# Front stage of a two-layer megakernel: ScalarE normalises, the next tile's x is transposed, differenced and mixed earlier, and the masked shifts are written with one tensor each

## The chip, the cores and the metric

The kernel runs on one core of a Trainium2 chip. Its engines are named as in the profile: PE (TensorE matrix multiplies), PEld (its weight loads), DVE (VectorE), ACT (ScalarE), POOL (GpSimd) and SP (SyncE, which here only issues DMAs). The metric is the device time of one execution in microseconds, median over runs.

## The reference

Two layers, each a sequence mixer beside a feed-forward part, on x of 4 x 512 tokens with 512 channels, all in float32. The change is in the front of layer 0, which computes for each batch entry:

```python
xn = (x - mean(x)) / sqrt(var(x) + 1e-5)                 # layer norm over 512 channels
delta = shifted(xn) - xn                                 # previous token minus this one
lr = tanh((xn + delta * mu_x) @ Wx1)                     # 512 -> 5 x 64
mus = einsum('btnr,hnr->btnh', lr, Wx2) + x_bias         # five mixes: r, w, k, v, g
r, k, v = ((xn + delta * m) @ W for m, W in ((mr, Wr), (mk, Wk), (mv, Wv)))
w = tanh((xn + delta * mw) @ Ww_a) @ Ww_b + bw           # decay: exp(-exp(w))
g = tanh((xn + delta * mg) @ Wg_a) @ Wg_b + bg           # gate
```

Beside it the front unpacks the 4-bit weights of layer 0's feed-forward part: every nibble is shifted into the sign and exponent bits of a float16, masked, and multiplied by its scale.

## The kernel before, in words

The function `front` goes over four tiles of 512 tokens (tile b is batch entry b; tile 0 and tile 3 are written out, 1 and 2 are a hardware loop). All five engines run their own program, `sequence(b)`, and meet only at semaphores: `signal.now(b, k)` is the k-th event of tile b, `before(b, k)` the same event one tile earlier. There is no scheduler; the order on each engine is the order of the code. So an engine that waits at one statement holds up all that is written behind it.

PE works through the list `jobs`, each job into one of eight PSUM banks in turn (`Ring`); a bank is free again when its reader has read it. A tile's jobs are: `xT` (16 transposes of the normalised x, four per bank, L706), `down` (of the tile before, L679), `low 1` (product with Wx1, from `x_mu`, L713), `decay` and `gate` (of the tile before, L683 and L688), `low 0` and `low 2`, 16 `mix` jobs for k, v, r and w (L719), `proj k` (L726), four `mix g`, `proj v`, `proj r`. In the second to fourth tile, down, decay and gate close the tile before.

What the others do for it, by lines of the profile:
- DVE: `statistics(b+1)` (L484 to L493), `unpack_gate_up(b, 1, 0)` for the first half of this tile's gate and up weights (L436 twice, L439, L455 twice), `evacuate` of the four g mixes (L508), `normalise(b+1)` (L500: four instructions that subtract the mean and multiply by `rstd`, into `xn`), `unpack_gate_up(b, 2, 1)` for the second half, `low_gate_up(b)` (L471: low part of the second half). Then, in the next tile, `x_mu = xT + delta * mu_x` (L535), the gate sums (L516), `unpack_down`, the gates (L526), and the 16 evacuations (L508).
- ACT: copies PSUM to `xT` (L631, four), tanh of down and low (L604, L639), decays, `project` of k (L598), `high_gate_up(b, 0)` (L591: rounded high part of the first half), `project` of v and r, `high_gate_up(b, 1)`.
- POOL: the differences `delta` (L402, four), the adds that finish 16 mixes (L396), `rstd` of the next tile (L389), the low part of the first half (L412), the adds for the four g mixes.
- SP: all loads and stores in one queue.

`x_mu` shares its memory with `mixed_v`, so it can be written only once proj v has been computed; `xT` can be overwritten only when all 20 adds of the tile before are done; `whole` is written again for the second half only when the low part of the first half has been made of it (`gu_lo_ready[0]`). A masked shift is one instruction with two tensor inputs, since the mask is read as a broadcast tensor.

Of the kernel before, what the change touches and what calls it, by code (L numbers as in the profile page):

```python
# [14 lines left out]
P = 128  # L15
# [114 lines left out]
def front(nc, w, x, spill, wgu, Wdn, relay, parts, ident, entry, constants, first_keys, first_values, Wx1, Wx2, low, hand,  # L130
# [17 lines left out]
    with ExitStack() as ctx:  # L148
# [22 lines left out]
        rstd = sb("rstd", [P, TT])  # L171

# [10 lines left out]
        shift = sb("shift", [P, 5], I32)  # L183
# [28 lines left out]
        rstd_ready = signal("rstd_ready", 1)  # L212
        xn_ready = signal("xn_ready", TT)
# [165 lines left out]
        def _(pool):  # L379
# [6 lines left out]

            def deviations(b):
                pool.wait_ge(*var_ready.now(b, 1))
                nc.gpsimd.tensor_tensor(rstd[:, :], veps[:, :], half[:, :], ALU.pow).then_inc(rstd_ready.sem, 1)  # L389
# [8 lines left out]
            def sequence(b, last=False):  # L398
                for kt in range(KT):

                    pool.wait_ge(*xT_ready.now(b, kt + 1))
                    nc.gpsimd.tensor_tensor(delta[:, kt, :], xT[:, kt, 1:T + 1], xT[:, kt, 2:T + 2],  # L402
                                            ALU.subtract).then_inc(delta_ready.sem, 1)
                add(b, mix_order[:4 * KT])
                if last:
                    add(b, mix_order[4 * KT:])
                else:
                    deviations(b + 1)
                n = J_LAST if last else JQ
# [5 lines left out]
                if not last:  # L415
                    add(b, mix_order[4 * KT:])

            deviations(0)
            with pool.Fori(0, B - 1) as b:
# [4 lines left out]
        def _(dve):  # L424
            for s in (stats_ready, mv_ready, var_ready, xn_ready, x_mixed, part_ready, unpack_step, unpacked,
# [3 lines left out]
            def unpack(b, n, words, shift_by, width):  # L429
# [2317 lines left out]
```

## Time and profile before

| | us |
|---|---|
| median of 3 runs | 1715.08 |
| lowest, highest | 1714.29, 1717.7 |
| time of the profiled execution | 1717.91 |
| its span, first to last instruction | 1716.1 |
| busy in it: PE, DVE, POOL, ACT | 1623.3, 1170.3, 615.8, 391.0 |
| front stage (to the first matmul of the next stage) | 259.8 |

The span is what the trace covers; the execution's own time is 1.8 us longer. Busy times are sums over all stages; what a change in the front is worth must be read from the front's own rows.

### The profile page before, as it was taken

The numbers are of one execution on the slowest core, as the hardware profiler recorded it, in microseconds if no ns is written. First come the engines' busy times: TensorE is split into PE (matmuls) and PEld (weight loads), VectorE is DVE, ScalarE is ACT, GpSimd is POOL, SyncE is SP. The second block draws the span as 40 slices with busy tenths as digits, with TensorE's granted clock in tenths as the row PEclk, the third lists the DMA queues.
The fourth block names the chain that finished last, engine by engine and source line by source line (L and its number), as shares of the span: only waits on it lengthen the run. The fifth ranks groups of instructions, "written<-read, shape, count | busy, mean of one in ns | idle before, by whom it ended". The sixth has DMA issues, their size and how long they took to land. (4 is left out here: it accounts for less than half of the span.)

```text
span 1716.1 us, 20281 instructions
## 1 busy us (share of the span) xinstructions
PE 1623.3 (95%) x6704; PEld 1128.9 (66%) x6704; DVE 1170.3 (68%) x1653; ACT 391.0 (23%) x670; POOL 615.8 (36%) x453
## 2 busy tenths in 40 slices
PE   6798898999999999989999999999998999999997
PEld 3343336646656656548877787877776667888886
DVE  5898876868878779746637877888777566251423
ACT  1222230011111110122323333343332222121211
POOL 3675563544564565451012222322322332010101
PEclk9999899999999999989999999999999999999999
DMA  5424558766666755513120000000003433101010
GB/s 193 170 101 171 207 186 266 234 215 202 220 211 201 231 201 201 189 43 117 44 80 26 19 21 18 25 19 19 19 1 136 159 103 116 52 25 73 19 55 25
DMA packets 84388, 197.87 MB, mean 115 GB/s; under 512 B 6864, under 2 KB 28112, under 8 KB 75984
## 3 DMA queue, kind: packets, MB, share of 16 engines
q1 hardware_dynamic: 84160, 196.28, 34.4%
q8 instruction: 47, 0.77, 0.2%
q10 hardware_dynamic: 144, 0.52, 0.1%
q14 instruction: 37, 0.30, 0.1%
HBM read 154.83 MB, written 41.94 MB: 115 GB/s over the span
## 5 line engine op out<-in xcount | busy, mean ns | idle before, releaser
L1926 DVE SCALAR_TENSOR_TENSOR l_acc<-l_ps,l_inv,l_acc 128x512 f32<-128x512 f32 x240 | 165.5, 747 | 10.2 <-PE l_ps L747 10.2
L2449 DVE CAST g_x_part<-g_x 128x512 fp32r<-128x512 f32 x64 | 36.6, 572 | 190.2 <-ACT g_x L2501 190.2
L1501 PE MATMUL r_ps<-Wdn,r_h 128*128 128x512 f32 x352 | 154.6, 595 | 0.1
L1037 POOL TENSOR_TENSOR r_rS<-r_S,r_rT 128x512 f32<-128x512 f32 x64 | 94.3, 1474 | 89.2 <-DVE r_S L1134 89.2
L1037 POOL TENSOR_TENSOR r_rS<-r_S,first_r 128x512 f32<-128x512 f32 x64 | 91.4, 1431 | 95.6 <-DVE r_S L1134 95.6
L1501 PEld LDWEIGHTS r_ps<-Wdn,r_h 128*128 128x128 f32 x352 | 65.7, 190 | 85.7 <-issue 84.6
L1804 POOL TENSOR_TENSOR relay<-l_expq,l_reluq 128x512 f32<-128x512 f32 x42 | 54.5, 1299 | 187.9 <-ACT l_expq L2084 187.9
L745 PE MATMUL r_ps<-relay_part,entry 128*128 128x512 f32 x256 | 106.0, 414 | 11.2 <-DVE r_h L1145 5.4
L2377 POOL TENSOR_TENSOR relay<-relay 128x512 f32<-128x512 f32 x16 | 21.7, 1356 | 257.5 <-DVE relay L2429 257.5
L1902 DVE TENSOR_SCALAR l_expq<-l_ps,l_bq 128x512 f32<-128x512 f32 x64 | 48.0, 751 | 85.9 <-ACT l_reluq L2080 85.9
L745 PE MATMUL l_ps<-l_M_part,l_sq_part 128*128 128x512 f32 x256 | 101.6, 397 | 3.9 <-DVE l_acc L1926 3.1
L745 PE MATMUL g_ps<-g_Wdn,g_x_part 128*128 128x512 f32 x256 | 103.7, 405 | 0.0
L746 PE MATMUL g_ps<-g_Wdn,g_x_part 128*128 128x512 f32 x256 | 101.2, 395 | 0.0
L747 PE MATMUL g_ps<-g_Wdn,g_x_part 128*128 128x512 f32 x256 | 101.2, 395 | 0.0
L746 PE MATMUL r_ps<-relay_part,entry 128*128 128x512 f32 x256 | 101.0, 395 | 0.0
L747 PE MATMUL r_ps<-relay_part,entry 128*128 128x512 f32 x256 | 100.9, 394 | 0.0
L747 PE MATMUL l_ps<-l_M_part,l_sq_part 128*128 128x512 f32 x256 | 99.9, 390 | 0.0
L746 PE MATMUL l_ps<-l_M_part,l_sq_part 128*128 128x512 f32 x256 | 99.6, 389 | 0.0
L2501 ACT ACTIVATE g_x<-g_ps,g_b_up 128x512 f32<-128x512 f32 x64 | 43.9, 685 | 210.2 <-PE g_ps L747 205.7
L2080 ACT ACTIVATE l_reluq<-l_ps,l_bq 128x512 f32<-128x512 f32 x64 | 44.1, 690 | 194.7 <-PE l_ps L747 194.6
L1134 DVE TENSOR_TENSOR_SCAN r_S<-first_w,r_ps 128x512 f32<-128x512 f32 x64 | 78.2, 1222 | 12.8 <-POOL r_rS L1037 10.8
L1359 ACT ACTIVATE r_tanh_gate<-r_ps 128x512 f32<-128x512 f32 x44 | 26.3, 597 | 262.5 <-PE r_ps L747 262.5
(321 smaller groups left out, 3993.5 us busy)
## 6 DMA issues: line engine op xcount, KB each, us to landing
entry<-scratch_wgu SPq DMA_DIRECT2D x32, 1024.0 KB, 5.5
V<-scratch_v SPq DMA_DIRECT2D x96, 256.0 KB
relay<-scratch_x SPq DMA_DIRECT2D x15, 1024.0 KB, 7.8
r_w_part<-scratch_wgu SPq DMA_DIRECT2D x12, 1024.0 KB, 8.4
scratch_wgu<-f_halves SPq DMA_DIRECT2D x24, 384.0 KB, 3.6
relay<-scratch_v SPq DMA_DIRECT2D x32, 256.0 KB
relay<-in_x SPq DMA_DIRECT2D x4, 1024.0 KB, 8.0
scratch_x<-f_xT SPq DMA_DIRECT2D x4, 1024.0 KB, 6.3
```

What stands on the lines that cost most here:

```text
L745: nc.tensor.matmul(out, left[1], right[0], start=start, stop=False)
L746: nc.tensor.matmul(out, left[0], right[1], start=False, stop=False)
L747: return nc.tensor.matmul(out, left[0], right[0], start=False, stop=stop)
L1037: nc.gpsimd.tensor_tensor(rS[u % RS][:, :], S[u % 2][:, 0:T], rT[u // DK][:, :], ALU.mult).then_inc(rS_ready.sem, 1)
L1134: nc.vector.tensor_tensor_scan(S[u % 2][:, 1:T + 1], dT[hh][:, :], kv, 0.0, ALU.mult, ALU.add).then_inc(S_ready.sem, 1)
L1501: last = nc.tensor.matmul(place[0][:, :], h[:, j, n * P:(n + 1) * P], Wdn[:, j, :], start=(j == 0), stop=(j == JT - 1))
L1804: nc.gpsimd.tensor_tensor(sq[i % N_SQ], expq[i % 2][:, :], reluq[i % 2][:, :], ALU.add).then_inc(sq_ready, 1)
L1902: nc.vector.tensor_scalar(expq[i % 2][:, :], place("q", i)[:, :], bq[:, h:h + 1], 0.0, ALU.add, ALU.min).then_inc(minq_ready, 1)
L1926: last = nc.vector.scalar_tensor_tensor(acc[b][:, t, :], ps, scale, acc[b][:, t, :], ALU.mult, ALU.add)
L2080: nc.scalar.activation(reluq[i % 2][:, :], place("q", i)[:, :], ACT.Relu, bias=bq[:, h:h + 1]).then_inc(reluq_ready, 1)
L2449: nc.vector.tensor_copy(hi[:, :], x2[j % 2][:, :]).then_inc(x2_hi_ready.sem, 1)
L2501: nc.scalar.activation(x2[j % 2][:, :], U.place(("up", j))[:, :], ACT.Relu, bias=b_up[:, j:j + 1]).then_inc(x2_ready.sem, 1)
```

## The change

`normalise` moves from DVE to ACT and becomes four activations `xn = rstd * x + offset`, with a new small DVE instruction `offset = -mean * rstd`. They stand behind `high_gate_up(b, 0)` and ahead of `project` of v and r. The four copies to `xT` and the tanh of `down` for tile b+1 move from the start of tile b+1 to before `high_gate_up(b, 1)`. On POOL, the four adds for g move ahead of the low part of the first half, `rstd` moves one add forward, and the four differences for tile b+1 follow that low part. On DVE, `x_mu` for tile b+1 moves ahead of `low_gate_up(b)`. In `unpack`, two masked shifts with a mask tensor each and their combination become a plain shift, a shift with an immediate mask (both with one tensor input), and a combination with an immediate mask; there is one more semaphore wait in it. The pieces of the diff are, in order, POOL's `sequence`, DVE's `unpack`, `normalise` and `sequence`, and ACT's `sequence`.

```diff
             def sequence(b, last=False):
-                for kt in range(KT):
-                    pool.wait_ge(*xT_ready.now(b, kt + 1))
-                    nc.gpsimd.tensor_tensor(delta[:, kt, :], xT[:, kt, 1:T + 1], xT[:, kt, 2:T + 2],
-                                            ALU.subtract).then_inc(delta_ready.sem, 1)
-                add(b, mix_order[:4 * KT])
-                if last:
-                    add(b, mix_order[4 * KT:])
-                else:
+                add(b, mix_order[:4 * KT - 1])
+                if not last:
                     deviations(b + 1)
+                add(b, mix_order[4 * KT - 1:])
...
                 rest.then_inc(gu_lo_ready[0].sem, 1)
                 if not last:
-                    add(b, mix_order[4 * KT:])
+                    deltas(b + 1)
...
             def unpack(b, n, words, shift_by, width):
-                for at, out in ((3, value), (4, shifted)):
-                    mask = shift[:, at:at + 1].bitcast(U32).broadcast_to([P, width])
-                    nc.vector.scalar_tensor_tensor(out[:, 0:width], words, shift_by, mask, ALU.logical_shift_left,
-                                                   ALU.bitwise_and).then_inc(unpack_step.sem, 1)
+                nc.vector.tensor_scalar(shifted[:, 0:width], words, shift_by, None,
+                                        ALU.logical_shift_left).then_inc(unpack_step.sem, 1)
+                dve.wait_ge(*unpack_step.now(b, 3 * n + 1))
+                nc.vector.tensor_scalar(value[:, 0:width], shifted[:, 0:width], 3, 0x0E000E00,
+                                        ALU.logical_shift_right, ALU.bitwise_and).then_inc(unpack_step.sem, 1)
                 dve.wait_ge(*unpack_step.now(b, 3 * n + 2))
-                nc.vector.scalar_tensor_tensor(value[:, 0:width], value[:, 0:width], 3, shifted[:, 0:width],
-                                               ALU.logical_shift_right,
+                nc.vector.scalar_tensor_tensor(value[:, 0:width], shifted[:, 0:width], 0x80008000,
+                                               value[:, 0:width], ALU.bitwise_and,
                                                ALU.bitwise_or).then_inc(unpack_step.sem, 1)
...
-            def normalise(b):
+            def offsets(b):
                 dve.wait_ge(*rstd_ready.now(b, 1))
-                dve.wait_ge(*ring.product_before(("xT", KT - 1), b))
-                for t in range(TT):
-                    nc.vector.scalar_tensor_tensor(xn[:, t, :], x_tok[:, t, :], mv[:, t, 0:1],
-                                                   rstd[:, t:t + 1].broadcast_to([P, C]), ALU.subtract,
-                                                   ALU.mult).then_inc(xn_ready.sem, 1)
+                dve.wait_ge(*xn_ready.before(b, TT))
+                nc.vector.scalar_tensor_tensor(offset[:, :], mv[:, :, 0], -1.0, rstd[:, :], ALU.mult,
+                                               ALU.mult).then_inc(offset_ready.sem, 1)
...
                 statistics(b + 1)
                 unpack_gate_up(b, 1, 0)
+                offsets(b + 1)
                 dve.wait_ge(*ring.product(("proj", "k", HH - 1), b))
                 evacuate(b, mix_order[4 * KT:])
-                normalise(b + 1)
                 unpack_gate_up(b, 2, 1)
+                mix_x(b + 1)
                 low_gate_up(b)
...
                 high_gate_up(b, 0)
+                normalise(b + 1)
                 project(b, "v")
                 project(b, "r")
+                copy_x(b + 1)
+                low_tanh(b + 1, lambda job: ring.product(job, b + 1), end_place)
                 high_gate_up(b, 1)
```

`mix_x` is the L535 loop and `copy_x` the L631 loop, unchanged in what they wait for. PE's and SP's orders are as they were.

The order on ACT, from the end of tile 0's proj k to the end of the tile, before (`f_outv`, `f_outr` are project of v and r):

```order
L591 ACTIVATE f_halves<-f_whole 128x3x256 [waits f_gu_stored1,f_unpacked]
L591 ACTIVATE f_halves<-f_whole 128x3x256
L598 ACTIVATE f_outv<-f_ps 128x512 [waits f_product,f_storedv]
L598 ACTIVATE f_outv<-f_ps 128x512 [waits f_product]
L598 ACTIVATE f_outr<-f_ps 128x512 [waits f_product,f_storedr]
L598 ACTIVATE f_outr<-f_ps 128x512 [waits f_product]
L591 ACTIVATE f_halves<-f_whole 128x3x256 [waits f_gu_stored0,f_unpacked]
L591 ACTIVATE f_halves<-f_whole 128x3x256
```

and of the change:

```order
L597 ACTIVATE f_halves<-f_whole 128x3x256 [waits f_gu_stored1,f_unpacked]
L597 ACTIVATE f_halves<-f_whole 128x3x256
L637 ACTIVATE f_xn<-relay,f_offset,f_rstd 128x512 [waits f_product,f_offset_ready]
L637 ACTIVATE f_xn<-relay,f_offset,f_rstd 128x512 x3
L604 ACTIVATE f_outv<-f_ps 128x512 [waits f_product,f_storedv]
L604 ACTIVATE f_outv<-f_ps 128x512 [waits f_product]
L604 ACTIVATE f_outr<-f_ps 128x512 [waits f_product,f_storedr]
L604 ACTIVATE f_outr<-f_ps 128x512 [waits f_product]
L645 ACTIVATE f_xT<-f_ps 128x512 [waits f_product,f_storedx,f_mix_ready]
L645 ACTIVATE f_xT<-f_ps 128x512 [waits f_product] x3
L610 ACTIVATE f_tlow<-f_ps 128x512 [waits f_product]
L597 ACTIVATE f_halves<-f_whole 128x3x256 [waits f_gu_stored0,f_unpacked]
```

The four activations into `f_xn` now stand between the first `f_halves` pair and project of v; the four `f_xT` copies and `f_tlow`, which belong to tile 1, stand ahead of the second pair. Before, they came behind it.

The order on DVE at the same place in tile 0, from the first half's `f_whole` on, before (`f_mixedk` here is the g mix, `f_mixedv` with L535 is `x_mu`):

```order
L455 SCALAR_TENSOR_TENSOR f_whole<-f_value,f_gu_scale 128x768 [waits f_gu_lo_ready1,f_unpack_step]
L455 SCALAR_TENSOR_TENSOR f_whole<-f_value,f_gu_scale 128x768
L508 SCALAR_TENSOR_TENSOR f_mixedk<-f_ps,f_col,relay 128x512 [waits f_product] x4
L500 SCALAR_TENSOR_TENSOR f_xn<-relay,f_mv,f_rstd 128x512 [waits f_product,f_rstd_ready]
L500 SCALAR_TENSOR_TENSOR f_xn<-relay,f_mv,f_rstd 128x512 x3
L436 SCALAR_TENSOR_TENSOR f_value<-f_gu_words,f_shift 128x768 [waits f_unpacked]
L436 SCALAR_TENSOR_TENSOR f_shifted<-f_gu_words,f_shift 128x768
L439 SCALAR_TENSOR_TENSOR f_value<-f_value,f_shifted 128x768 [waits f_unpack_step]
L455 SCALAR_TENSOR_TENSOR f_whole<-f_value,f_gu_scale 128x768 [waits f_gu_lo_ready0,f_unpack_step]
...
L471 TENSOR_TENSOR f_halves<-f_whole,f_halves 128x3x256 [waits f_gu_hi_ready]
```

and of the change:

```order
L460 SCALAR_TENSOR_TENSOR f_whole<-f_value,f_gu_scale 128x768 [waits f_gu_lo_ready1,f_unpack_step]
L460 SCALAR_TENSOR_TENSOR f_whole<-f_value,f_gu_scale 128x768
L504 SCALAR_TENSOR_TENSOR f_offset<-f_mv,f_rstd 128x4 [waits f_xn_ready,f_rstd_ready]
L519 SCALAR_TENSOR_TENSOR f_mixedk<-f_ps,f_col,relay 128x512 [waits f_product] x4
L438 TENSOR_SCALAR f_shifted<-f_gu_words,f_shift 128x768 [waits f_unpacked]
L441 TENSOR_SCALAR f_value<-f_shifted 128x768 [waits f_unpack_step]
L444 SCALAR_TENSOR_TENSOR f_value<-f_shifted,f_value 128x768 [waits f_unpack_step]
L460 SCALAR_TENSOR_TENSOR f_whole<-f_value,f_gu_scale 128x768 [waits f_gu_lo_ready0,f_unpack_step]
...
L512 SCALAR_TENSOR_TENSOR f_mixedv<-relay,f_col,f_xT 128x512 [waits f_delta_ready,f_product]
L512 SCALAR_TENSOR_TENSOR f_mixedv<-relay,f_col,f_xT 128x512 [waits f_delta_ready] x3
L476 TENSOR_TENSOR f_halves<-f_whole,f_halves 128x3x256 [waits f_gu_hi_ready]
```

The four L500 instructions are gone for one 128x4 instruction, and `x_mu` of tile 1 (L512) stands between the second half's `f_whole` and its low part; before, it came first in the next tile's program, behind that low part.

The order on POOL in the loop over tiles 0 to 2, before, from the last add for w (`f_mixedw`) on:

```order
L396 TENSOR_TENSOR f_mixedw<-f_mixedw,f_xT 128x512 [waits f_part_ready]
...
L389 TENSOR_TENSOR f_rstd<-f_veps,f_half 128x4 [waits f_var_ready]
...
L412 TENSOR_TENSOR f_halves<-f_whole,f_halves 128x3x256 [waits f_gu_hi_ready]
L412 TENSOR_TENSOR f_halves<-f_whole,f_halves 128x3x256
...
L396 TENSOR_TENSOR f_mixedk<-f_mixedk,f_xT 128x512 [waits f_part_ready]
```

and of the change, from the last add for r (`relay`) on; the second last line of dots stands for the other three g adds, the rest for what only sets registers:

```order
L405 TENSOR_TENSOR relay<-relay,f_xT 128x512 [waits f_part_ready]
...
L398 TENSOR_TENSOR f_rstd<-f_veps,f_half 128x4 [waits f_var_ready]
...
L405 TENSOR_TENSOR f_mixedw<-f_mixedw,f_xT 128x512 [waits f_part_ready]
...
L405 TENSOR_TENSOR f_mixedk<-f_mixedk,f_xT 128x512 [waits f_part_ready]
...
L415 TENSOR_TENSOR f_halves<-f_whole,f_halves 128x3x256 [waits f_gu_hi_ready]
L415 TENSOR_TENSOR f_halves<-f_whole,f_halves 128x3x256
...
L393 TENSOR_TENSOR relay<-f_xT 128x512 [waits f_xT_ready]
```

The g adds (`f_mixedk`) now stand ahead of the low part of the first half (`f_halves`), and the differences (`relay<-f_xT`) of the next tile right behind it; before, the differences came first in the next tile's program.

## Rows read from the trace of the kernel before

**Rows 1.** busy time in three stretches: length, engines, granted clock, DMA share, GB/s
```profile
0.00:260.00 260.00, 212.57 (x625) 95.39 (x626) 207.95 (x244) 60.62 (x101) 150.42 (x118) 0.93 0.49 173
126.00:129.00 3.00, 2.79 (x13) 2.56 (x13) 3.00 (x3) 0.00 (x0) 3.00 (x2) 0.56 1.04 368
139.00:143.00 4.00, 4.00 (x5) 1.51 (x6) 3.20 (x3) 0.00 (x0) 1.99 (x2) 0.50 1.03 344
```

**Rows 2.** waits of PE in 0 to 262 us: total us, times, longest
```profile
PE f_ps L706 <- DVE f_xn L500: 18.7, 9, 12.1
PE f_ps L713 <- DVE f_mixedv L535: 17.3, 4, 5.8
PE f_ps L679 <- POOL f_mixedk L396: 4.0, 3, 2.4
```

**Rows 3.** timeline of PE: start us, duration us, what, idle before and releaser
```profile
100.76 7.13 PE L726 MATMUL f_ps<-f_mixedk,f_W 128*128 128x512 f32 x16
...
116.72 7.03 PE L726 MATMUL f_ps<-relay,f_W 128*128 128x512 f32 x16
...
126.21 2.98 PE L706 MATMUL f_ps<-ident,f_xn 128*128 128x128 f32 x13 [1.34 <-DVE f_xn L500]
129.19 0.90 PE L679 MATMUL f_ps<-f_mixedw,f_W 128*64 128x512 f32 x1
...
138.80 5.97 PE L713 MATMUL f_ps<-f_mixedv,Wx 128*128 128x512 f32 x8 [5.68 <-DVE f_mixedv L535]
144.70 0.69 PE L683 MATMUL f_ps<-f_tlow,f_Wb 64*128 64x512 f32 x1
...
153.69 1.13 PE L719 MATMUL f_ps<-low,Wx 64*128 64x512 f32 x4
...
223.17 7.13 PE L726 MATMUL f_ps<-f_mixedk,f_W 128*128 128x512 f32 x16
```

**Rows 4.** timeline of DVE, same columns
```profile
84.80 1.61 DVE L516 TENSOR_TENSOR f_g<-f_ps,f_bg 128x256 f32<-128x256 f32 x4 [3.40 <-PE f_ps L688]
...
91.10 1.29 DVE L526 SCALAR_TENSOR_TENSOR f_gate<-f_tanhg,f_g 128x512 f32<-128x512 f32 x2
...
108.21 1.92 DVE L436 SCALAR_TENSOR_TENSOR f_value<-f_gu_words,f_shift 128x768 uint32<-128x768 uint32 x1
...
116.56 2.71 DVE L508 SCALAR_TENSOR_TENSOR f_mixedk<-f_ps,f_col,relay 128x512 f32<-128x512 f32 x4
119.20 6.96 DVE L500 SCALAR_TENSOR_TENSOR f_xn<-relay,f_mv,f_rstd 128x512 f32<-128x512 f32 x4
...
134.53 2.67 DVE L471 TENSOR_TENSOR f_halves<-f_whole,f_halves 128x768 fp32r<-128x768 f32 x2 [1.72 <-ACT f_halves L591]
137.13 5.08 DVE L535 SCALAR_TENSOR_TENSOR f_mixedv<-relay,f_col,f_xT 128x512 f32<-128x512 f32 x4
```

**Rows 5.** timeline of POOL, same columns
```profile
118.41 4.03 POOL L412 TENSOR_TENSOR f_halves<-f_whole,f_halves 128x768 fp32r<-128x768 f32 x2 [1.77 <-ACT f_halves L591]
122.40 6.64 POOL L396 TENSOR_TENSOR f_mixedk<-f_mixedk,f_xT 128x512 f32<-128x512 f32 x4
135.06 5.93 POOL L402 TENSOR_TENSOR relay<-f_xT 128x512 f32<-128x512 f32 x4 [6.02 <-ACT f_xT L631]
```

**Rows 6.** timeline of ACT, same columns
```profile
14.60 1.28 ACT L631 ACT_TABLE_LOAD   x1 [14.60 <-PE f_ps L706]
...
116.75 1.58 ACT L591 ACTIVATE f_halves<-f_whole 128x768 fp32r<-128x768 f32 x2 [8.22 <-DVE f_whole L455]
...
134.41 2.04 ACT L631 ACTIVATE f_xT<-f_ps 128x512 f32<-128x512 f32 x4
```

**Rows 7.** groups of DVE by form: busy us, mean ns, idle before
```profile
L1875 DVE TENSOR_SCALAR l_expq<-l_reluq 128x512 f32<-128x512 f32 x16 | 6.8, 427 | 0.5
...
L436 DVE SCALAR_TENSOR_TENSOR f_value<-f_dn_words,f_shift 128x768 uint32<-128x768 uint32 x3 | 3.0, 1008 | 0.0
```

**Rows 8.** DMA issues on the page: KB each, us to landing
```profile
scratch_wgu<-f_halves SPq DMA_DIRECT2D x24, 384.0 KB, 3.6
```

More of the change, by code:

```diff
@@ L171, in front @@
         rstd = sb("rstd", [P, TT])
+        offset = sb("offset", [P, TT])
         xT = sb("xT", [P, KT, T + 2])
@@ L182, in front @@
         dn_scale = sb("dn_scale", [P, DQ, C], F16)
-        shift = sb("shift", [P, 5], I32)
+        shift = sb("shift", [P, 3], I32)
         shifted = sb("shifted", [P, GQ], U32)
@@ L385, in _, with deltas @@
                 s.ahead(pool)
+            def deltas(b):
+                for kt in range(KT):
+                    pool.wait_ge(*xT_ready.now(b, kt + 1))
+                    nc.gpsimd.tensor_tensor(delta[:, kt, :], xT[:, kt, 1:T + 1], xT[:, kt, 2:T + 2],
+                                            ALU.subtract).then_inc(delta_ready.sem, 1)
             def deviations(b):
@@ L493, in statistics, with mix_x @@
                 nc.vector.tensor_tensor(veps[:, :], mv[:, :, 1], eps[:, :], ALU.add).then_inc(var_ready.sem, 1)
[L495 removed]
+            def offsets(b):
                 dve.wait_ge(*rstd_ready.now(b, 1))
[L498 to L502 removed]
+                dve.wait_ge(*xn_ready.before(b, TT))
+                nc.vector.scalar_tensor_tensor(offset[:, :], mv[:, :, 0], -1.0, rstd[:, :], ALU.mult,
+                                               ALU.mult).then_inc(offset_ready.sem, 1)
+            def mix_x(b):
+                dve.wait_ge(*ring.product_before(("proj", "v", HH - 1), b))
+                for kt in range(KT):
+                    dve.wait_ge(*delta_ready.now(b, kt + 1))
+                    nc.vector.scalar_tensor_tensor(x_mu[:, kt, :], delta[:, kt, :], mu_x[:, kt:kt + 1],
+                                                   xT[:, kt, 2:T + 2], ALU.mult, ALU.add).then_inc(x_mixed.sem, 1)
             def evacuate(b, mixes):
@@ L530, in sequence @@
             def sequence(b, first=False, last=False):
-                dve.wait_ge(*ring.product_before(("proj", "v", HH - 1), b))
-                for kt in range(KT):
-                    dve.wait_ge(*delta_ready.now(b, kt + 1))
-                    nc.vector.scalar_tensor_tensor(x_mu[:, kt, :], delta[:, kt, :], mu_x[:, kt:kt + 1],
-                                                   xT[:, kt, 2:T + 2], ALU.mult, ALU.add).then_inc(x_mixed.sem, 1)
                 if not first:
@@ L570, in _ @@
             statistics(0)
-            normalise(0)
+            offsets(0)
             dve.wait_ge(small_loaded, 4 * 16)
+            mix_x(0)
             sequence(0, first=True)
@@ L624, in decays, with normalise, copy_x @@
                                          scale=-1.0).then_inc(out_ready["w"].sem, 1)
-            def sequence(b, first=False, last=False):
+            def normalise(b):
+                act.wait_ge(*offset_ready.now(b, 1))
+                act.wait_ge(*ring.product_before(("xT", KT - 1), b))
+                for t in range(TT):
+                    nc.scalar.activation(xn[:, t, :], x_tok[:, t, :], ACT.Identity, bias=offset[:, t:t + 1],
+                                         scale=rstd[:, t:t + 1]).then_inc(xn_ready.sem, 1)
+            def copy_x(b):
                 act.wait_ge(*mix_ready.before(b, N_MIX))
@@ L632, in sequence @@
                                          ACT.Copy).then_inc(xT_ready.sem, 1)
-                if not first:
-                    low_tanh(b, lambda job: ring.product(job, b), end_place)
+            def sequence(b, first=False, last=False):
                 for m in LOWS:
```

13 lines of the change are left out of this document (8 added, 5 removed).

## Prediction

> **What bounds the kernel now.** I read first how busy each engine is in the front stage: PE works 212.6 of its 260 us, DVE 208.0 [rows 1]. Neither is full, so the question is which waits end late. The list of PE's waits names them: 18.7 us for `xn` (12.1 of them once, at the start), 17.3 us for `x_mu`, 4.0 us for POOL's adds for g [rows 2]. Behind the front the change touches nothing, and the next stage opens when PE, ACT and the last stores are through, so what PE gains in the front moves the end of the kernel by as much.
>
> Where the waits lie shows in PE's timeline from tile 1 to tile 2. I count from K = 100.76, the start of proj k of tile 1, in us after K. Proj r ends at +23.0; the transposes wait 1.34 for `xn`, down starts at +28.4, PE then idles 5.68 and gets `x_mu` from +38.0 on, and the decay job starts at +43.9 [rows 3]. K to K is 61.2 (100.76 to 223.17 over two tiles) [rows 3].
>
> Why is `x_mu` late? The chain back, on DVE: `x_mu` 137.13 to 142.21, behind the low part of the second half, behind its `whole`, behind `normalise`, 6.96 us, behind evacuate g, behind `whole` of the first half [rows 4]. ACT's `xT` copies come at 134.41, though the transposes that they read were ready some microseconds before, because `high_gate_up(b, 1)` stands ahead of them and waits for DVE [rows 6]. So the next tile's x goes through the tail of this one. During PE's long idle the clock falls: in 139 to 143 us PE is granted 0.50 (1.2 of 2.4 GHz), and eight low-1 rows take 5.97 us, where sixteen rows of proj r, at a full clock, take 7.03 [rows 1, 3].
>
> **What a DVE instruction costs beside POOL.** A masked shift with two tensors takes 1.01 us in the down unpack, when POOL is idle, and 1.92 us at 108.21, when POOL adds [rows 4, 7]. So beside POOL each DVE instruction with two SBUF tensors waits about one POOL instruction, 0.9 to 1.0 us, and POOL waits for DVE likewise: its four g adds take 6.64 us beside `normalise` [rows 5].
>
> **The change, part by part, in the new order.**
>
> *Unpack.* The trace has no shift with one tensor at this width. The nearest row is a one-tensor multiply-add of 512 columns from SBUF, 0.427 us [rows 7]. For 768 columns I scale to 0.5 to 0.64 and take 0.56; the other bound is 1.01, no gain. Beside POOL I add the same wait, so 1.5 instead of 1.9 for two of three steps: the first unpack gains 0.8 us, and the end of `whole` moves from +15.8 (116.56) to +15.0 [rows 4]. The extra semaphore wait is at most 0.1.
>
> The Trainium skill speaks against counting more. "SBUF — State Buffer", section "Who interferes with whom", says that a `tensor_scalar` in a two-port mode takes the port pair shared with GpSimd for the whole instruction, and the later one blocks fully; only a one-input instruction outside these modes runs past POOL. The lockstep of rows 4 and 5 agrees for two tensors; no row here shows it for one. If one-tensor shifts ran past POOL at 0.56, the g chain below would start some 1.9 us earlier and the sum would be 5 to 6 us larger.
>
> *Offset.* A 128x4 instruction, no row of this size: 0.2, up to 1.1 if it meets a POOL add. POOL should be waiting for the g mixes then; I take 0.2. Evacuate g, 2.71 us from PSUM, ends at +18.0 [rows 4].
>
> *Normalise on ACT.* Four 128x512 activations: below, the four `xT` copies, 2.04; above, twice the pair of 768 columns, 1.58, so 3.2 [rows 6]. I take 2.3. They follow `high_gate_up(b, 0)`, which starts as `whole` is done and takes 1.58, so `xn` is ready by about +19.2, ahead of proj r's end at +23.0. Queued behind them is `project` of v and r, two copies each, done for v by +20.3; PE needs those banks from +24. The cover is 3 us, so the move costs PE nothing, and DVE is rid of 6.96 us. PE transposes +23.0 to +26.0 (2.98 at a reduced clock), and ACT copies `xT` behind it, the last at about +26.6.
>
> *POOL.* The g adds now go first: they follow evacuate g from +16.0, two free at 1.1, two beside the second unpack, and end at about +21.5. That releases down, which now runs straight behind the transposes, +26.0 to +29.9 (129.19 to 133.12 before) [rows 3]. Then the low part of the first half, 4.03 before beside `normalise`, now 3.8: done at +25.3, 3.6 later than before (+21.7) [rows 5]. This is what is late next: DVE comes to `whole` of the second half at about +22.5 and waits there until +25.3, and behind it stand `x_mu`, the low part, the gate sums. `mix_x` waits for POOL's differences, queued behind the same low part.
>
> *From +25.3 to `x_mu`.* Before, the low part (2 x 768 columns) and `x_mu` ran beside the four differences, from 134.53 to 142.21: 7.68 us, differences 5.93 of it [rows 4, 5]. Now the same picture with `whole` in place of the low part: the last `x_mu` is done at +33.0. PE then needs its last two low-1 rows. Before, decay began 2.5 us after the last `x_mu`, at the halved clock; PE now idles in pieces of 1 us or less, so I take the full clock and 1.0. Decay starts at +34.0 instead of +43.9. One boundary gains 9.9, and there are three: 29.7.
>
> *Is the rest of the tile ready for it?* From decay to the first mix PE takes 9.0 (144.70 to 153.69), so mix starts at +43.0 [rows 3]. DVE must do the low part (2.67), gate sums (from +36.0), down unpack and gates. From sums to the end of gates it took 7.6 (84.80 to 92.39) [rows 4], minus 0.9 for one-tensor shifts: +42.7. Just covered, by 0.3 plus the microsecond before the first mix can be evacuated; if shifts stay at 1.01, the cover is gone and each tile loses under 1 us. ACT's `high_gate_up(b, 1)` needs the stores of the first half: issued from +25.3, four of 384 KB, 3.6 us to landing each [rows 8], overlapping, so +31 to +33, about when its `tlow` is done.
>
> *First tile.* The activation table load, 1.28 us, ran after the first transposes, on the way to `xT` [rows 6]. In the new order it stands ahead of `normalise`, while DVE still takes statistics. ACT's `xn` costs there what DVE's did. I take 1.2. *Last tile.* PE's wait for the g adds, 2.4 us [rows 2], shrinks as they meet shorter shifts: 0.8 (0 to 1.2).
>
> Sum: 29.7 + 1.2 + 0.8 = 31.7. The profiled execution took 1717.91, its span 1716.1, so 1686.2 and 1684.4; the median lies 2.8 below it, at 1715.08, which gives 1683.4.
>
> **Rivals.**
>
> *The chain is longer.* The low part, the differences and `x_mu` come in strict turns (1.0 for POOL, 0.95 or 0.7 for DVE), shifts stay at 1.01, and PE's clock still halves in its smaller idle pieces. For it: after an idle of only 1.34, PE was granted 0.56 in 126 to 129, and thirteen transposes took 2.98 [rows 1, 3]. Price: 0.9, up to 1, and 1.5 us a boundary, 1.5 to 4 together, 5 to 12 in all: a gain of 20 to 27, 1688 to 1695.
>
> *PE-bound.* POOL and DVE slip past each other and `x_mu` no longer waits. Then decay comes at 23.0 + 3.0 + 3.9 + 3.5 (eight rows at a full clock) = +33.4, or +32 if transposes run at a full clock too: 10.5 to 12 a boundary, a gain of 34 to 38, 1677 to 1681. Against it: the lockstep in rows 4 and 5.
>
> *The wait only moves.* The copies to `xT` wait for all 20 adds of the tile and `mix_x` for POOL's low part, so if POOL comes 8 us late (g adds starting after +24), the gain is nearly gone: 1705 to 1715. Against it: evacuate g hangs only on proj k's end, +7, and on the first unpack.
>
> *Slower.* ACT waits at `high_gate_up(b, 1)` for the first half's stores, and behind it stand the tanh of low 1, which the k and v mixes need, and gate tanh. Stores are now issued 3.6 us later. Cover ends when they land at +40.8 (mix at +43, less 1.6 and 0.6 of ACT); each microsecond more costs one, and past +50.7 a tile is slower than before: 25 us from issue to landing against 3.6. At +52 the time would be 1.3 a boundary above, less 2.0: 1717.
>
> **How the numbers follow.** Chances: my forecast, a gain of 27 to 34, 0.45; longer chain 0.32; PE-bound 0.12; the wait only moves 0.07; slower 0.04. The forecast is that of the likeliest, 1683.4, its own range 1681 to 1688. For 8 in 10 I take the two neighbours in: 1677 to 1697. About 0.2% (3.4 us) is what a measurement of this kernel tells from no change. Faster by more 0.94, within 0.02, slower 0.04.
>
> **What the profile of the changed kernel would show.** PE's wait for `xn` down to its first, 12 us, and for `x_mu` under 2 us a tile; K to K 51 to 52; granted clock 1.00 where low 1 runs; the shift instructions at 0.5 to 0.65 alone and about 1.5 beside POOL; DVE idle some 3 us for POOL's low part before `whole` of the second half; one table load, hidden. The prediction fails if that idle is much longer, if one-tensor shifts cost POOL more than they save DVE, or if evacuation of the mixes starts late after PE's first mix.

## The result, and the profile after

The changed kernel took 1691.8 us (median of 4 runs, 1687.62 to 1692.92), before 1716.39 (4 runs): the ratio is 0.984, 95% interval 0.982 to 0.986, 24.6 us less. That is inside the range of 1677 to 1697 and 8.4 us above the forecast of 1683.4, so outside the forecast's own 1681 to 1688; it falls into the 1688 to 1695 of the rival "the chain is longer". Two more sets of timings of the changed kernel gave 1688.9 (ratio 0.982, interval 0.979 to 0.985) and 1688.5 (0.982, 0.980 to 0.984), against medians of before of 1718.0 and 1720.0: 29.1 and 31.5 us less.

Busy time in stretches of after; the columns are those of [rows 1].

```profile
0.00:232.00 232.00, 201.83 (x625) 90.37 (x626) 178.00 (x232) 72.34 (x117) 140.48 (x118) 0.99 0.54 194
68.00:72.00 4.00, 3.11 (x4) 1.45 (x5) 3.95 (x5) 1.58 (x2) 1.64 (x2) 0.57 1.05 365
122.00:126.00 4.00, 3.74 (x6) 1.36 (x6) 3.46 (x5) 1.58 (x2) 0.50 (x1) 0.63 1.03 346
176.00:180.00 4.00, 3.74 (x11) 1.55 (x12) 3.78 (x5) 2.01 (x3) 0.08 (x1) 1.00 1.01 346
```

The front now ends at 231.77, the start of the first matmul of the recurrence, where before stood 259.80: 28.0 us less. DVE is rid of 30 us of busy time and stands at 178.0 where [rows 1] has 207.95. The last three lines are the same piece of work in the three boundaries between tiles, low 1: its granted clock is 0.57 and 0.63 in two of them and 1.00 in the third.

PE's waits in the front of after (total, times, longest):

```profile
PE f_ps L726 <- ACT f_xn L637: 13.0, 4, 12.3
PE f_ps L733 <- DVE f_mixedv L512: 8.4, 7, 2.9
PE f_ps L699 <- POOL f_mixedk L405: 0.6, 1, 0.6
```

Of the wait for `xn` only the one at the start is left, that for `x_mu` is half of what [rows 2] shows, that for the g adds is nearly gone. PE's timeline from tile 0 to tile 1 (K = 37.69), and low 1 in the second boundary (K = 91.23) and in the third (K = 144.80):

```profile
37.69 7.13 PE L746 MATMUL f_ps<-f_mixedk,f_W 128*128 128x512 f32 x16
...
60.51 1.91 PE L726 MATMUL f_ps<-ident,f_xn 128*128 128x128 f32 x16
...
68.89 5.14 PE L733 MATMUL f_ps<-f_mixedv,Wx 128*128 128x512 f32 x8 [2.88 <-DVE f_mixedv L512]
73.96 0.69 PE L703 MATMUL f_ps<-f_tlow,f_Wb 64*128 64x512 f32 x1
...
121.75 1.10 PE L733 MATMUL f_ps<-f_mixedv,Wx 128*128 128x512 f32 x2 [2.21 <-DVE f_mixedv L512]
123.11 4.50 PE L733 MATMUL f_ps<-f_mixedv,Wx 128*128 128x512 f32 x6 [0.26 <-DVE f_mixedv L512]
...
175.33 1.10 PE L733 MATMUL f_ps<-f_mixedv,Wx 128*128 128x512 f32 x2 [2.22 <-DVE f_mixedv L512]
176.69 2.84 PE L733 MATMUL f_ps<-f_mixedv,Wx 128*128 128x512 f32 x6 [0.26 <-DVE f_mixedv L512]
```

The transposes run without a wait at the full clock (1.91 for sixteen, where [rows 3] has 2.98 for thirteen). The idle for `x_mu` is 2.88 and not 5.68, and eight rows of low 1 take 5.14, part of them at the half clock (3.60 is the full clock); in the second boundary six rows take 4.50, in the third 2.84. Decay starts at K+36.3 where [rows 3] has +43.9. DVE and POOL in the same boundary:

```profile
45.69 1.52 DVE L438 TENSOR_SCALAR f_shifted<-f_gu_words,f_shift 128x768 uint32<-128x768 uint32 x1
...
53.44 2.71 DVE L519 SCALAR_TENSOR_TENSOR f_mixedk<-f_ps,f_col,relay 128x512 f32<-128x512 f32 x4
...
63.88 3.41 DVE L460 SCALAR_TENSOR_TENSOR f_whole<-f_value,f_gu_scale 128x768 f32<-128x768 f16 x2 [3.56 <-POOL f_halves L415]
67.22 4.29 DVE L512 SCALAR_TENSOR_TENSOR f_mixedv<-relay,f_col,f_xT 128x512 f32<-128x512 f32 x4
...
76.71 0.61 DVE L438 TENSOR_SCALAR f_shifted<-f_dn_words,f_shift 128x768 uint32<-128x768 uint32 x1
77.36 0.56 DVE L441 TENSOR_SCALAR f_value<-f_shifted 128x768 uint32<-128x768 uint32 x1
```

```profile
54.26 5.24 POOL L405 TENSOR_TENSOR f_mixedk<-f_mixedk,f_xT 128x512 f32<-128x512 f32 x4 [1.63 <-DVE f_mixedk L519]
59.46 4.32 POOL L415 TENSOR_TENSOR f_halves<-f_whole,f_halves 128x768 fp32r<-128x768 f32 x2
63.73 5.91 POOL L393 TENSOR_TENSOR relay<-f_xT 128x512 f32<-128x512 f32 x4
```

Read them together: POOL works from 54.26 to 69.64 without a gap. DVE has done its share at 60.3 and idles 3.56 for POOL's low part, and `x_mu` ends 1.9 us behind the last difference, at 71.51, K+33.8.

### The profile page after: what moved, and what is told of

It reads as the page before. It is cut to its first block and busy times, and to the rows that moved or that the text cites. A ratio compares the mean times of both kernels' runs of the same rounds, so it can differ in the third digit from the quotient of the medians.

```text
span 1691.1 us, 20299 instructions
## 1 busy us (share of the span) xinstructions
PE 1614.6 (95%) x6704; PEld 1124.4 (66%) x6704; DVE 1139.8 (67%) x1641; ACT 402.4 (24%) x686; POOL 605.4 (36%) x453
## 3 DMA queue, kind: packets, MB, share of 16 engines
q1 hardware_dynamic: 84160, 196.28, 34.7%
## 5 line engine op out<-in xcount | busy, mean ns | idle before, releaser
L2100 ACT ACTIVATE l_reluq<-l_ps,l_bq 128x512 f32<-128x512 f32 x64 | 44.1, 690 | 194.8 <-PE l_ps L767 194.7
```

Of the source, the lines that this page charges most:

```text
L2100: nc.scalar.activation(reluq[i % 2][:, :], place("q", i)[:, :], ACT.Relu, bias=bq[:, h:h + 1]).then_inc(reluq_ready, 1)
```

## The experiments

My theory after this reading: the boundary hangs on POOL's chain (g adds, low part, differences), and the idle that it leaves PE costs twice, since the clock then halves on low 1. The rivals: DVE's own load sets `x_mu`; and what was lost behind the front (1459.4 us from the first recurrence matmul to the end, where before has 1456.3) is a cost of the change. The table has what the traces show. "Decay" is the start of the decay job in us after K, in the three boundaries; "front ends" is the first matmul of the recurrence, "behind it" the rest of the traced execution.

| kernel | decay | K to K | front ends | behind it | median (runs) |
|---|---|---|---|---|---|
| before | 43.9 43.9 44.1 | 61.1 61.1 61.3 | 259.8 | 1456.3 | 1716.4 (4) |
| after | 36.3 36.3 34.7 | 53.5 53.6 51.8 | 231.8 | 1459.4 | 1691.8 (4) |
| after_again | 36.5 36.3 34.7 | 53.8 53.6 51.9 | 232.7 | 1454.3 | 1688.9 (4) |
| after_third | 36.3 36.3 34.7 | 53.6 53.6 51.9 | 231.7 | 1454.4 | 1688.5 (5) |
| shifts_only | 43.3 42.4 42.8 | 60.5 59.6 60.0 | 255.4 | 1453.9 | 1712.3 (10) |
| normalise_only | 39.6 39.6 38.9 | 56.7 56.8 56.1 | 244.4 | 1456.9 | 1697.3 (4) |
| moves_only | 39.5 37.9 37.6 | 56.8 55.2 54.8 | 242.1 | 1452.8 | 1697.8 (4) |
| low_on_dve | 33.6 32.8 32.8 | 50.9 50.1 50.0 | 224.8 | 1458.4 | 1683.9 (4) |
| low_on_dve_again | 33.6 32.8 32.9 | 50.9 50.1 50.0 | 225.0 | 1458.4 | 1686.1 (6) |
| deltas_first | 33.0 33.0 33.0 | 57.1 57.3 55.7 | 244.9 | 1458.3 | 1702.7 (4) |
| keep_busy | 36.2 36.2 36.2 | 53.4 53.4 53.4 | 234.1 | 1452.3 | 1688.8 (4) |
| keep_busy_short | 35.3 34.7 34.6 | 52.6 51.9 51.8 | 230.6 | 1456.2 | 1689.2 (5) |

**The changed kernel again.** No edit, twice.

> The changed kernel once more, beside before on one chip: does the gain repeat, and where does the loss behind the front come from? If the 3.0 us that the later stages took longer in the profile of after are a cost of the change, first matmul of the recurrence at 231.8 us and 1459.3 us behind it stand again. If they are half-clock pieces of 3.4 us that fall on other work from one execution to the next, the front repeats within 0.5 us and the part behind it comes out anywhere from 1455 to 1460, with the half-clock stretches at other places or at the same distance from the start of the execution. Time 1686 to 1693.

> The changed kernel once more, for the part behind the front, next to low_on_dve_again on one chip. If the later stages carry no cost of the change, the part behind the first matmul of the recurrence falls between 1452 and 1460 us as in all kernels so far, in no order with the edits; front 231.5 to 233.

The first repeat had the front at 232.7, 0.9 off, the second at 231.7. Behind the front the same kernel took 1459.4, 1454.3 and 1454.4, and all kernels together lie between 1452.3 and 1459.4, in no order with their edits. So the 3.0 us "lost" in the first profile are scatter, which blurs differences of 3 to 5 us between medians. Where the question is the front, I therefore read its end from the traces, which repeats within 0.9.

**The shifts alone**, on the kernel before (shortened; the combination behind them also takes its mask as an immediate):

```
-for at, out in ((3, value), (4, shifted)):
-    scalar_tensor_tensor(out, words, shift_by, mask, shift_left, and)
+tensor_scalar(shifted, words, shift_by, None, shift_left)
+tensor_scalar(value, shifted, 3, 0x0E000E00, shift_right, and)
```

> Only the unpack's two masked shifts are put in one-tensor form, on the kernel before; nothing is moved. My theory (every DVE instruction beside POOL waits about one POOL instruction, alone the form takes 0.56 in place of 1.01): in the boundary the first unpack ends 0.8 us earlier and the second unpack 0.8 to 1.6, so x_mu comes 1.5 to 2.4 us earlier, three times, 5 to 7 us faster in all; down unpack 0.56 a step. Rival, that the one-tensor form holds the port against POOL or is held by it for longer than one of its instructions: a step beside POOL takes 2 us or more and the kernel is 0 to 2 us faster, or slower; POOL's adds get longer.

The front ended 4.4 us earlier, less than the 5 to 7 expected; the ratio is 0.998, interval 0.996 to 0.999. The steps went as priced, 0.6 alone and 1.3 to 1.5 beside POOL, but the last `x_mu` ended 1.6, 0.7 and 1.6 us earlier in the three boundaries, where 1.5 to 2.4 were expected in each, and decay came 0.6, 1.5 and 1.3 earlier.

**The normalisation alone on ScalarE**, offset on DVE, everything else where it was:

```
-                normalise(b + 1)      # DVE, four of 128x512
+                offsets(b + 1)        # DVE, one of 128x4
+                normalise(b + 1)      # ACT, behind high_gate_up(b, 0)
```

> On the kernel before, only the normalisation goes to ScalarE (offset on DVE); copies, differences and mixes stay where they were, shifts too. By the chain of the kernel before, DVE is rid of 6.96 us ahead of the second unpack, but POOL's low part and g adds then take turns with that unpack: x_mu comes 4 to 6 us earlier, since ACT's copies of xT stand behind the second high half; the wait for xn goes (1.3 a boundary). Decay at +38 to +40 in place of +43.9: gain 4 to 6 a boundary, 1.2 in the first tile, 13 to 19 in all. Rival, that the order ahead of the high half is what matters and DVE's load is not: under 6 us in all.

The front is 15.4 us shorter, inside the expected 13 to 19; ratio 0.988, interval 0.986 to 0.990. This one piece brings over half of the whole gain. Its list of PE's waits names what comes next, the g adds:

```profile
PE f_ps L689 <- POOL f_mixedk L398: 15.4, 4, 5.2
```

**All but the shifts.**

> All of the change but the shifts: normalise on ScalarE, copy, differences and mix ahead, with the masked shifts on two tensors as before. If x_mu hangs on the chain POOL's g adds, low part, differences (my theory), the second unpack's longer shifts hide in DVE's idle of 3.6 us and only the first unpack moves the chain, by 0.8 us, and the down unpack by 0.9 before the gates: 1 to 2 us a boundary more than after, and the last tile gets back up to 0.9 us at the handoff: 2 to 5 us slower than after, gain over before 19 to 23 us. Rival, DVE's own load sets x_mu: all three unpacks count, 3 us a boundary, 9 us slower than after, gain 15 to 16.

It missed: the front ended 10.4 us later than in after, not 2 to 5, and the median is 9 us higher. That is the rival's number, but its mechanism is not there. DVE's idle for POOL's low part is as long as in after, so the second unpack's longer shifts do hide:

```profile
66.90 3.41 DVE L459 SCALAR_TENSOR_TENSOR f_whole<-f_value,f_gu_scale 128x768 f32<-128x768 f16 x2 [3.58 <-POOL f_halves L415]
70.24 4.29 DVE L511 SCALAR_TENSOR_TENSOR f_mixedv<-relay,f_col,f_xT 128x512 f32<-128x512 f32 x4
```

```profile
56.48 6.03 POOL L405 TENSOR_TENSOR f_mixedk<-f_mixedk,f_xT 128x512 f32<-128x512 f32 x4 [1.63 <-DVE f_mixedk L518]
```

With K = 39.10, `x_mu` ends at +35.4, 1.6 later than in after: 0.8 through the first unpack and 0.8 because the g adds meet longer shifts (6.03 where after has 5.24), a term that I had left out. And the half clock now covers all of low 1 in the first boundary (0.50 in 72 to 76, eight rows in 6.75) and comes in the third as well, where eight rows take 5.57:

```profile
71.91 6.75 PE L732 MATMUL f_ps<-f_mixedv,Wx 128*128 128x512 f32 x8 [4.50 <-DVE f_mixedv L511]
```

```profile
72.00:76.00 4.00, 4.00 (x5) 1.68 (x6) 3.97 (x5) 1.58 (x2) 0.66 (x1) 0.50 1.01 332
```

So decay is 3.2, 1.6 and 3.0 us later, the last tile takes 1.1 more, and K of tile 0 came 1.4 later, of which after's own repeats show 0.6 as scatter. The shifts are worth 4.4 us alone and 10.4 on top of the moves.

Beside normalise_only this run also shows how little the other moves bring by themselves: the front ends 2.2 us earlier (242.1 for 244.4) and the medians are the same. `x_mu` ends at +35.4 in the first boundary where normalise_only has +38.0, but there PE waited for the g adds instead and ran low 1 behind them without a wait for `x_mu` (eight rows in 3.70); here it idles 4.50 and runs them in 6.75. So the pieces add up to 15.4 + 2.2 + 10.4 = 28.0 in this order; what the moves are worth once the shifts are short, no run has alone.

**POOL relieved of the low part** in tiles 0 to 2:

```
 # POOL                                 # DVE, between unpack's steps and whole
-    low part of the first half
     deltas(b + 1)                     +    low part of the first half
```

> The changed kernel, but in tiles 0 to 2 VectorE makes the low part of the first half, in the 3.6 us in which it idled between the second unpack's steps and its whole; POOL goes from the g adds straight to the differences. My theory (x_mu hangs on POOL's chain of g adds, low part, differences): the low part ends at K+24.5 in place of +26.1, whole at +28, x_mu at +32.2 in place of +33.8; PE idles 1.2 us, its clock stays up, decay starts at +33.3 in place of +36.3, +36.3, +34.7; K to K 50.3; 5 to 8 us faster than after. Rival, that VectorE's own load sets x_mu: the idle is filled and nothing moves, decay at +36 and the time within 2 us of after.

> The best version so far against the changed kernel on one chip. The front ended 7.4 us earlier in its trace (first matmul of the recurrence at 224.8 for 231.8 and 232.7); the same here within 1 us, median 1680 to 1685 and 5 to 9 us below that of after_third. If its earlier time came from the part behind the front, the medians lie within 3 us of each other.

DVE and PE of low_on_dve, K = 38.66:

```profile
61.32 1.83 DVE L484 TENSOR_TENSOR f_halves<-f_whole,f_halves 128x768 fp32r<-128x768 f32 x2
63.18 3.39 DVE L461 SCALAR_TENSOR_TENSOR f_whole<-f_value,f_gu_scale 128x768 f32<-128x768 f16 x2
66.49 4.30 DVE L520 SCALAR_TENSOR_TENSOR f_mixedv<-relay,f_col,f_xT 128x512 f32<-128x512 f32 x4
```

```profile
68.16 1.10 PE L741 MATMUL f_ps<-f_mixedv,Wx 128*128 128x512 f32 x2 [1.19 <-DVE f_mixedv L520]
69.52 2.84 PE L741 MATMUL f_ps<-f_mixedv,Wx 128*128 128x512 f32 x6 [0.26 <-DVE f_mixedv L520]
```

The low part ends at +24.5, `x_mu` at +32.1, PE idles 1.19 at a granted clock of 1.00, decay starts at +33.6: each step as expected, within 0.3. DVE carries 5.6 us more in this front (183.56 of 225, where after has 178.00) and everything comes earlier, which the rival excludes. The front ends 6.9 us before that of after; against before the ratio is 0.980, interval 0.978 to 0.983. The medians show less against after: 1683.9 beside keep_busy's 1688.8, and 1686.1 beside 1688.5 for after on the same chip, 2.4 less where I expected 5 to 9. Of the difference, 4.0 us lie behind the front (1458.4 and 1454.4), where this kernel has no other code than after. Medians within 3 us were to be the sign that the earlier time came from behind the front, and the two traces of this kernel contradict that: their fronts end at 224.8 and 225.0. Over all timings on this chip this kernel's ten average 1685.0 and after's five 1688.8. The gain in the front is shown; how much of it the whole kernel keeps is not settled by these runs.

**Differences first**: POOL makes the differences before the low part, DVE mixes x before `whole`.

> The changed kernel with the next x ahead of more: POOL makes the differences before the low part of the first half, and VectorE mixes x between the second unpack's steps and its whole. x_mu is done by +29.5, before PE has ended down (+28.3) and one row more: PE never waits for it, decay at +32.3. But the low part of the first half ends at +32.5 in place of +26.1, its stores land at +38 to +39, and ScalarE's second high half waits there, with the tanh of low 1 and VectorE's low part, gate sums and unpack behind it. By my reading of the stores' cover (they may land as late as +40.8) this costs 1 to 4 us of the 4 gained a boundary: K to K 50 to 54, time from 5 us faster than after to 3 slower. If PE's waits moved to mixed g, k and v (evacuation starts late), the cover of the stores is smaller than I said.

Decay came at +33.0, near the +32.3 expected, and yet K to K rose to 57.1, outside the 50 to 54. ACT, DVE and PE of this kernel, K = 39.20:

```profile
78.96 1.58 ACT L597 ACTIVATE f_halves<-f_whole 128x768 fp32r<-128x768 f32 x2 [10.80 <-DMA scratch_wgu<-f_halves]
...
83.18 1.28 ACT L616 ACTIVATE f_tanhg<-f_g 128x512 f32<-128x512 f32 x2 [2.17 <-DVE f_g L528]
...
85.33 0.69 ACT L625 ACTIVATE f_expw<-f_ps,f_col 128x512 f32<-128x512 f32 x1
```

```profile
80.57 1.83 DVE L477 TENSOR_TENSOR f_halves<-f_whole,f_halves 128x768 fp32r<-128x768 f32 x2 [5.93 <-ACT f_halves L597]
82.31 1.41 DVE L528 TENSOR_TENSOR f_g<-f_ps,f_bg 128x256 f32<-128x256 f32 x4
...
89.87 0.74 DVE L520 SCALAR_TENSOR_TENSOR f_mixedk<-f_ps,f_col,relay 128x512 f32<-128x512 f32 x1
```

```profile
81.21 1.13 PE L739 MATMUL f_ps<-low,Wx 64*128 64x512 f32 x4
86.07 10.34 PE L739 MATMUL f_ps<-low,Wx 64*128 64x512 f32 x28 [3.73 <-ACT f_expw L625]
```

The stores of the first half are issued at 72.80 (+33.6) and have landed by +39.8, before the +40.8 that the prediction named as the end of their cover. But behind the second high half stands more than its tanh. DVE's low part waits for it (idle 5.93), and behind that stand gate sums, down unpack and gates; DVE's first evacuation comes at 89.87, 9.3 us after the start of its low part, and the sixteen then follow without a pause. ACT's gate tanhs wait for the gate sums, and behind them stands the exp that frees a bank for PE's mixes, which go on at +46.9 after a wait of 3.7. That wait is not what counts: PE had made the first two mixes from +42.0 on, and DVE took them up only at +50.7. The cover has to be counted along this chain. By an estimate from these rows, with one us lost for each that the second high half is late, the cover ended near +33 (39.8 less the 6.9 us that this tile lost, worked out below), about where the second high half stands in after, +32.3. The kernel is 14 us slower than after by the medians, 13 in the front.

**PE kept at work** while `x_mu` is late, with matmuls whose result is overwritten (five in keep_busy, two in keep_busy_short; shortened):

```
+if n == LOWS[0] and not first:
+    for _ in range(5):
+        matmul(place, W[:, 0, 0:P], W[:, 0, 0:T], start=True, stop=True)
```

> The changed kernel, with five matmuls 128x512 more ahead of low 1 in tiles 1 to 3 (weights times weights into low 1's own bank, which the real product then overwrites), so that PE works 2.2 us of its 2.2 to 2.9 us idle. If the half clock on low 1 in boundaries 1 and 2 comes from PE's idle, the granted clock stays 1.00 there, eight rows of low 1 take 3.5 to 4 us, decay starts at +34.7 in all three boundaries and K to K is 51.8 to 52 each: 3.4 us faster than after in the front. If the half clock does not depend on that idle, the rows stay at 5.1 us for eight and nothing is gained, or up to 0.5 us a boundary is lost.

> As keep_busy, but two matmuls more ahead of low 1 in place of five: in keep_busy five took 4.56 us (each of them two passes of 0.45) and held low 1 until +32.6, past PE's idle, so that decay stood at +36.2 although the clock stayed at 1.00. Two take 1.8 us of the 2.2 to 2.9 of idle. If idle sets the clock: 1.00 over the whole front, low 1 ends at +34.7 and decay starts there in all three boundaries, K to K 51.9 each, 3.3 us less than after in the front. If 0.4 to 1.1 us of idle are enough to halve it: decay at +36.3 in the first two boundaries as in after.

```profile
67.01 4.56 PE L731 MATMUL f_ps<-f_W 128*128 128x512 f32 x10
71.41 3.60 PE L736 MATMUL f_ps<-f_mixedv,Wx 128*128 128x512 f32 x8
```

```profile
0.00:232.00 232.00, 212.31 (x654) 95.69 (x654) 177.98 (x232) 72.34 (x117) 140.25 (x115) 1.00 0.53 190
```

and of keep_busy_short:

```profile
0.00:230.00 230.00, 206.58 (x636) 91.87 (x636) 178.11 (x232) 72.39 (x117) 140.56 (x118) 1.00 0.54 195
```

In keep_busy a matmul has two rows in the timeline, so five took 4.56 us and outlasted the idle; that was my error. The clock stayed at 1.00 over the whole front and eight rows of low 1 took 3.60 instead of 5.14, but decay did not come earlier, and in the third boundary it came 1.5 later. With two matmuls (1.98 us) the clock was 1.00 as well, decay stood at +35.3, +34.7, +34.6, and K to K was 52.6, 51.9, 51.8: 2.5 us less than after over the three, where I expected 3.3 (the front ends 1.2 us earlier, since K of tile 0 came 1.4 later). So the half clock on low 1 comes from PE's idle, and it costs after 0.9 and 1.6 us in two boundaries. Nor is it chance: the changed kernel showed it in the same two boundaries in all three traces. Why the same idle of 2.2 us halves the clock in the second boundary and not in the third, no run here tells.

**What a shift costs beside an add**, without the rest of the kernel.

> Only a measurement; it computes nothing of the reference. Six POOL adds of 128x512 with two tensors back to back (in two of ten phases each waits for the one before it), and beside them three masked shifts 128x512 of VectorE, in one-tensor form in half of the phases and in two-tensor form in the other; then three shifts with POOL idle. My pricing, a wait of one POOL instruction for each shift: each takes 1.4 to 1.7 us beside POOL in either form, 0.43 and 0.75 alone, and POOL's six adds take 9 to 10 us in place of 6.6. Rival from the last tile of after, where one shift took 6.03 us and ended with the last of POOL's adds: while POOL has a next add that waits for nothing, VectorE gets no turn at all; its first shift then takes 6 us or more, the others 0.43 or 0.75, and POOL's adds 1.15 each; where each add waits for the one before, the shifts slip between.

> Only a measurement; it computes nothing of the reference. In each of 48 stretches POOL runs six adds of 128x512 back to back and VectorE, after 0 to 23 memsets of one column (about 0.06 us each, to shift its start against POOL's), one masked shift 128x512, waits for it, and a second one; one-tensor form in every other stretch. In the side_by_side run no shift was held for more than one add. If the stall of 6.03 us in the last tile is a matter of where in POOL's add the shift starts, some stretches show a shift of 3 to 7 us that ends with POOL's last add, in both forms; if it needs something else of the last tile, all take 0.43 to 1.8 us.

```profile
10.04 1.28 DVE L2739 TENSOR_SCALAR m_alone<-m_words,m_mask 128x512 uint32<-128x512 uint32 x3 [8.63 <-POOL m_m L2714]
11.36 2.08 DVE L2744 SCALAR_TENSOR_TENSOR m_alone<-m_words,m_mask 128x512 uint32<-128x512 uint32 x3
13.61 5.17 DVE L2744 SCALAR_TENSOR_TENSOR m_two<-m_words,m_mask 128x512 uint32<-128x512 uint32 x3 [0.18 <-POOLq L2719]
...
24.63 4.37 DVE L2739 TENSOR_SCALAR m_one<-m_words,m_mask 128x512 uint32<-128x512 uint32 x3 [0.18 <-POOLq L2719]
```

Alone a shift takes 0.43 with one tensor and 0.69 with two; beside POOL 1.46 and 1.72, so about 1.03 more in both forms. POOL's six adds took 7.90 beside one-tensor shifts and 8.70 beside two-tensor ones, less than the 9 to 10 expected. The rival, a shift that is held for all six adds, did not come. The scan shows of what the 1.03 consist. POOL's adds begin at 34.94 in one stretch and at 377.67 in another; one shift starts with an add, the other inside one:

```profile
34.95 2.94 DVE L2735 TENSOR_SCALAR m_one<-m_words,m_mask 128x512 uint32<-128x512 uint32 x2
...
378.26 0.95 DVE L2735 TENSOR_SCALAR m_one<-m_words,m_mask 128x512 uint32<-128x512 uint32 x1
...
379.25 1.37 DVE L2735 TENSOR_SCALAR m_one<-m_words,m_mask 128x512 uint32<-128x512 uint32 x1
```

The first shift's time falls with each step of its start, from 1.54 at an add's start to 0.95 when it comes 0.6 into it, and it ends 0.28 us behind the end of that add (a two-tensor shift 0.55) wherever it began: a shift waits for the rest of the add that it meets and then runs. In 48 stretches none took more than 1.81 us.

## Why the prediction held, and where its sum was off

The predicted gain was 31.7 us; the front gained 28.0. The largest part of what is missing is the half clock of the rival "the chain is longer"; its other terms, shifts that stay at 1.01 and stricter turns for the differences and `x_mu`, did not come. PE-bound is out, since PE still waits for `x_mu`, and so is "the wait only moves": the g adds start at +16.6, not after +24.

**Held.** The chain and its members came as forecast: the first unpack's `whole` ends at +15.8 (forecast +15.0), evacuate g at +18.5 (+18.0), the g adds at +21.8 (+21.5), down runs straight behind the transposes, DVE idles 3.56 (some 3). From the low part's end to the last `x_mu` it is 7.7 us, as said. From decay to the next K it is 17.2 (17.3 forecast): the rest of the tile was ready, and ScalarE's second high half, at +32.3, did not hold it up. Shifts take 0.61 and 0.56 (0.56) alone and 1.52 and 1.33 (1.5) beside POOL; the table load is hidden. Normalise on ScalarE was estimated at 2.3 and took 2.92, within its cover.

**The step that failed** is the term "decay starts at +34.0, full clock and 1.0". It measured +36.3, +36.3 and +34.7, so the three boundaries gained 24.6 instead of 29.7, and K to K was 51 to 52 in the third alone. Of the 5.2 by which decay was late in all, 1.1 lies ahead of the last `x_mu`, which ended at +33.8, +33.1 and +33.2 (forecast +33.0; the low part took 4.32, not 3.8). The other 4.1 lie between it and decay: 2.5, 3.2 and 1.5 us in place of 1.0. Of them 1.5 are the term itself, which is 1.5 a boundary at the full clock too, as the third boundary and all three of keep_busy_short show; 2.6 are the half clock. PE's idle was not "in pieces of 1 us or less" but 2.88, 2.21 and 2.22 ahead of low 1, with the half clock on low 1 in two of three: 5.14 us for eight rows where 3.60 is the full clock. The forecast had down end at +29.9 with the slowed transposes of [rows 3]; with no wait for `xn` they took 1.91, down ended at +28.3, and PE stood idle 1.6 us sooner. I had seen in [rows 1, 3] that 0.56 was granted behind an idle of 1.34, and put it into the rival only.

**Small terms.** The first tile gained 2.0 (forecast 1.2; one repeat 1.4), and from the last K to the end of the front it is 35.1 us where before has 36.6, 1.5 less (forecast 0.8): 24.6 + 2.0 + 1.5 = 28.1, the front's 28.0. These two hide 1.5 of the 5.1 us missing in the boundaries, which is luck: the first tile's share is no more than it scatters.

**The medians** came out 24.6, 29.1 and 31.5 us lower in three comparisons. What that differs from the front's 28.0 lies behind the front, as far as the traces show, where the same code takes between 1452 and 1459 us.

**The weight on the unpack.** The prediction gave the shifts 0.8 us a boundary on the chain. moves_only shows 1.6 on the chain and, in two of three boundaries, 1.4 to 1.6 again through the clock. On the Trainium skill's rule ("SBUF — State Buffer", section "Who interferes with whom"), that a `tensor_scalar` in a two-port mode and GpSimd block each other fully: side_by_side and scan agree, the one-tensor shift waits as the two-tensor one does (1.03 more in both forms; whether it ran in such a mode no row says), so the larger sum that I had set against it is out.

**The slower rival** rested on a cover of the stores up to +40.8 and 25 us from issue to landing. deltas_first shows it too generous: issued at +33.6 and landed by +39.8, they went with a K to K of 57.1, where decay at +33.0 and the 17.2 behind it would give 50.2: 6.9 us a tile.

## What to carry to other kernels

Where several engines share a chain across a loop boundary, take from the profile which engine runs through it without a gap, and give the one that idles in it (here DVE, 3.56 us) a link of the chain; it moved the front by 6.9 us, and `normalise` handed to ScalarE moved it by 15.4. A microsecond of TensorE's idle in front of work that is on the path can cost two (in moves_only `x_mu` 1.6 late made decay 3.2 late), because the next rows may run at the half clock; so put that case into the sum, not only into a rival. And count the cover of a transfer to the last engine that stands behind it in program order.

## What the runs showed of the hardware that was not expected

In the last tile the first shift behind evacuate g took 6.03 us and ended with the last of POOL's four adds; this is DVE and POOL of after:

```profile
207.58 6.03 DVE L438 TENSOR_SCALAR f_shifted<-f_gu_words,f_shift 128x512 uint32<-128x512 uint32 x1
213.64 0.43 DVE L441 TENSOR_SCALAR f_value<-f_shifted 128x512 uint32<-128x512 uint32 x1
```

```profile
207.51 1.28 POOL L405 TENSOR_TENSOR f_mixedw<-f_mixedw,f_xT 128x512 f32<-128x512 f32 x1
208.73 4.59 POOL L405 TENSOR_TENSOR f_mixedk<-f_mixedk,f_xT 128x512 f32<-128x512 f32 x4
```

DVE got no turn in five adds. I first put it down to the one-tensor form, and that fell: moves_only and normalise_only, with two tensors, took 6.30 at this place, and every kernel here but the one before did so (there 1.75, 1.57 and 1.64, with 6.38 for the adds). Nor is it the start against POOL's add: the shift begins 0.05 to 0.08 us after an add does, in the kernel before too, and in deltas_first, where it begins 0.84 after, it takes 6.50 all the same; in the scan a start of 0.06 gives 1.48 and 1.75. What decides it stays open. It costs DVE little, since the following steps then run alone (8.5 us from the shift to the end of `whole`, where before has 8.1), and it gives PE its g adds 1.8 us sooner.
